# Products with V of a group's last 52 keys: two stationary tiles in place of three, and new orders of work in blocks 1 to 6

## The chip, the cores and the metric

The kernel runs on one core of a Trainium2 chip. Its time is the device time of one execution in microseconds (us). TensorE (PE in the profile) multiplies matrices. VectorE (DVE), ScalarE (ACT) and GpSimd (POOL) do elementwise work. SyncE (SP) issues most of the DMAs. Each engine runs its own instructions in the order in which they are written, and a wait on a semaphore holds everything queued behind it on that engine.

## What is computed

A block of Flamingo in float32: `x` is 2 batches of 2048 rows of 512, the context is 2 batches of 77 keys.

```python
x = x + tanh(g_xattn) * xattn(layernorm(x), ctx, ctx, Wq, Wk, Wv, Wo)   # 16 heads of 32, 77 keys
x = x + tanh(g_ffn)   * ffn(layernorm(x), w_gate, w_up, w_down)         # silu(gate) * up, hidden 1536
# in xattn: q @ k.T * 32**-0.5, key k masked for query rows below k, softmax, @ v, @ Wo.T
```

## The kernel before

The 4096 rows are worked on in 8 blocks of 512 rows (n = 0 to 7), each of four tiles of 128 rows (t = 0 to 3). After the blocks comes the feed-forward part in four pairs of steps, which the change does not touch. A float32 operand is split into a high part, which ScalarE copies out of PSUM as fp32r, and a low part, the difference, which VectorE forms. A product takes three TensorE products: high by high, low by high, high by low (`CROSS`).

One step n of the attention interleaves three things on TensorE, in this order: scores of tile 0; `values` for four groups m of four heads (the product of V with the probabilities of block n-1); scores of tile 1; then for each tile the transposes of its probabilities in three pieces `p(n, t, r)`, r = 0, 1, 2; `o(t)`, the projection of `values` by Wo; and at the end `q(m)`, the queries of block n+1. Scores are computed in two units of eight heads; unit 0 is softmaxed by VectorE (`shift0`: largest, then the difference) and ScalarE (`exp0`), unit 1 by ScalarE straight out of PSUM with a bias (`largest1`, `offset1` on VectorE, then eight instructions `exp1`). VectorE then forms sums and reciprocals (`denominator0`, `denominator1`), and GpSimd multiplies by them (`weigh`). Only then can TensorE transpose.

The eight heads of a unit have 616 keys in a row. They are transposed in five chunks, the third of which holds the last 52 keys of the even group and the first 52 of the odd group. A group's product with V therefore has three chunks, each with three TensorE products: nine per group, 36 per block. The pieces r of a transposed tile are chunks 0 to 3, 4 to 7 and 8 to 9 of the ten of both units. Piece r = 2 is 128 x 256 and is copied by one ScalarE instruction (`p_high`, L780) and subtracted by one VectorE instruction (`p_low`, L1070), which then frees the bank (`t_free`). `values` (L1646) waits for `t_free` before it reads the pieces: group 0 for all but the last two pieces of block n-1, group 1 for all but the last, groups 2 and 3 for all.

Two PSUM banks alternate for `values`, `o` and `q` (`m_wait`, semaphore `m_free`), two for the transposes (`t_wait`, `t_free`). `values` of group m + 2 waits until `weighted(m)` on ScalarE and `v_low(m)` on VectorE have emptied its bank, and `o(3)` waits for `residual(1)` on VectorE.

The orders of ScalarE, VectorE and GpSimd in a step are written out by hand (`step` at L882 and L1296, `block` at L630). Steps 1 to 6 share them, steps 0 and 7 have their own (`first_block`, `last_step`). Layer-norm statistics of later blocks (`stats`, `stats2`) are placed among VectorE's work by `st(i)`: in step 1 eight of them for blocks 2 and 3, in steps 2 to 5 four, in step 6 eight for the feed-forward part.

V is built in block 0. SyncE issues small DMAs, one for each entry of `V_PLACES` and batch, that put 25 to 77 rows of V where their chunk has them (L424). `v_high(b)` on ScalarE (L764) waits for all DMAs of its batch. In `first_block` of ScalarE `v_high(1)` stands between `p(2, 2)` and `q(2)`, and `p(3, 0)` comes behind `q(2)`.

At the end of step 7 ScalarE does `p(3, 0)`, `xv_copy`, `p(3, 1)`, `b12_copy`, `p(3, 2)`, and TensorE goes on with `values` for block 7.

## Time and profile before

| | |
|---|---|
| median of 3 runs | 872.54 us (872.40 to 872.73) |
| the profiled execution | 872.86 us, of which the span of the profile is 871.0 us |
| PE busy | 855.0 us, 98% |
| DVE, ACT, POOL busy | 653.3 us (75%), 461.1 us (53%), 403.1 us (46%) |

The page gives the busy time of each engine, the span in 40 slices, and the chain of work that ended last, followed back from the last instruction. The trace gives each instruction with its start and length, and behind it in brackets how long its engine stood idle before it and what ended that. A line of the timeline can merge instructions that follow each other on the engine (x2, x12); its length is then that of the whole.

### The profile page before, as it was taken

The page shows a single profiled execution, that of the slowest core. Times are in us where ns is not written, and L with a number is a line of the kernel's source. Part 1 is how long each engine was busy: PE and PEld are TensorE (multiplying, and loading weights), DVE is VectorE, ACT ScalarE, POOL GpSimd, SP SyncE. Part 2 cuts the span into 40 slices and gives each one's busy share as a digit, 9 for nine tenths or more (in the row PEclk, how much of TensorE's full clock was granted, in tenths as well). Part 3 has the DMA queues.
Part 4 walks back from the last instruction along what each step waited for, and adds up shares of the span by engine and source line. Part 5 has one row for each costly group of instructions (what it writes and reads, how often), then busy time and mean ns, then how long its engine had stood idle before and what let it go on. Part 6 is the DMA issues. An engine that isn't in the chain of part 4 may idle for free.

```text
span 871.0 us, 12870 instructions
## 1 busy us (share of the span) xinstructions
PE 855.0 (98%) x4087; PEld 706.8 (81%) x4087; DVE 653.3 (75%) x1081; ACT 461.1 (53%) x1130; POOL 403.1 (46%) x344
## 2 busy tenths in 40 slices
PE   8999999999999999999999999999999999999997
PEld 6678888888888887888888888888888888888876
DVE  5988877777786878679688478788487887587882
ACT  5787575756666757546056265165363364461550
POOL 4664555555565665437144444155253256151250
PEclk9999999999999999999999999999999999999999
DMA  9233847272728131567333256043275143243202
GB/s 329 78 107 121 270 153 253 84 241 85 242 97 277 48 133 38 212 234 266 116 120 135 97 187 248 14 165 122 74 247 187 48 164 107 96 171 117 90 38 98
DMA packets 60406, 128.73 MB, mean 148 GB/s; under 512 B 7616, under 2 KB 20416, under 8 KB 60352
## 3 DMA queue, kind: packets, MB, share of 16 engines
q1 hardware_dynamic: 58960, 125.95, 41.9%
q10 hardware_dynamic: 1392, 2.10, 0.7%
q8 instruction: 29, 0.48, 0.2%
q14 instruction: 25, 0.20, 0.1%
HBM read 99.93 MB, written 27.79 MB: 147 GB/s over the span
## 4 chain that ended last, share of the span: by engine, by line
PE 86%; DVE 6%; ACT 3%; issue 1%; DMA 1%; POOL 1%; ACTq 0%; DVEq 0%
PE psum L1880 34%; PE psum L1591 20%; PE psum L1930 18%; PE psum L1660 9%; PE psum L1616 4%; DMA xs<-x_t 1%; PE psum L1704 1%; ACT e L800 1%; POOL hT L705 1%; DVE bn L1055 1%; DVE K L1149 1%; DVE mx L1105 1%; DVE e L1097 0%; DVE qT L1079 0%; DVE mx L1094 0%
## 5 line engine op out<-in xcount | busy, mean ns | idle before, releaser
L1880 PE MATMUL psum<-xv,ring 128*128 128x512 f32 x1344 | 308.0, 390 | 1.0 <-ACT a L985 0.7
L1880 PEld LDWEIGHTS psum<-xv,ring 128*128 128x128 f32 x1344 | 251.3, 188 | 55.1 <-ACT a L985 1.1
L705 POOL TENSOR_TENSOR hT<-th,hT 128x512 fp32r<-128x512 f32 x48 | 86.7, 1806 | 200.7 <-ACT hT L1005 200.7
L1930 PE MATMUL psum<-w_d,hT 128*128 128x512 f32 x768 | 177.7, 390 | 1.3 <-POOL hT L705 0.8
L1930 PEld LDWEIGHTS psum<-w_d,hT 128*128 128x128 f32 x768 | 143.6, 188 | 32.7 <-POOL hT L705 2.0
L554 POOL TENSOR_TENSOR e<-e,rden 128x616 f32<-128x616 f32 x64 | 78.0, 1219 | 110.4 <-DVE rden L1131 75.2
L800 ACT ACTIVATE e<-psum,nmx,q_scale 128x77 f32<-128x77 f32 x256 | 102.9, 428 | 3.1 <-DVE nmx L1111 3.1
L973 ACT ACTIVATE a<-psum 128x512 f32<-128x512 f32 x48 | 28.7, 599 | 131.6 <-PE psum L1880 131.4
L1471 DVE SCALAR_TENSOR_TENSOR acc<-psum,gate_ffn,acc 128x512 f32<-128x512 f32 x64 | 47.6, 749 | 65.1 <-PE psum L1930 65.1
L1660 PE MATMUL psum<-wo,aT 128*128 128x512 f32 x384 | 95.5, 398 | 0.5 <-DVE aT L1079 0.5
L1591 PE MATMUL psum<-xT,wq 128*128 128x512 f32 x360 | 89.1, 398 | 0.4 <-DVE qT L1079 0.4
L1660 PEld LDWEIGHTS psum<-wo,aT 128*128 128x128 f32 x384 | 69.8, 188 | 14.3 <-DVE aT L1079 0.8
L1591 PEld LDWEIGHTS psum<-xT,wq 128*128 128x128 f32 x360 | 65.5, 188 | 14.7 <-DVE qT L1079 1.9
L705 POOL TENSOR_TENSOR hT<-c,hT 128x512 fp32r<-128x512 f32 x48 | 62.3, 1297 | 22.2 <-ACT hT L1005 22.2
L1591 PE MATMUL psum<-pT,V 128*128 128x512 f32 x288 | 68.0, 392 | 0.6 <-DVE aT L1079 0.6
L773 ACT ACTIVATE pT<-psum 128x512 fp32r<-128x512 f32 (+1 forms) x96 | 49.7, 534 | 33.9 <-PE psum L1616 33.9
L1591 PE MATMUL psum<-K,qT 128*128 128x308 f32 x384 | 63.9, 310 | 0.9 <-ACT e L800 0.9
L1591 PEld LDWEIGHTS psum<-pT,V 128*128 128x128 f32 x288 | 53.3, 188 | 12.5 <-DVE aT L1079 1.1
L1435 DVE SCALAR_TENSOR_TENSOR th<-th,c 128x512 f32<-128x512 f32 x48 | 56.1, 1168 | 7.1 <-ACT th L998 4.3
L1591 PEld LDWEIGHTS psum<-K,qT 128*128 128x128 f32 x384 | 56.9, 188 | 5.4 <-ACT e L800 1.8
L1005 ACT ACTIVATE hT<-th 128x512 fp32r<-128x512 f32 x48 | 30.4, 633 | 54.2 <-DVE th L1448 54.2
L1068 DVE TENSOR_TENSOR pT<-psum,pT 128x512 fp32r<-128x512 f32 (+1 forms) x96 | 55.7, 588 | 2.6 <-ACT pT L773 0.9
(110 smaller groups left out, 1204.7 us busy)
## 6 DMA issues: line engine op xcount, KB each, us to landing
ring<-w_var SPq DMA_DIRECT2D x48, 896.0 KB, 4.6
w_var<-stage SPq DMA_DIRECT2D x12, 896.0 KB, 4.6
x_ln<-x SPq DMA_DIRECT2D x32, 256.0 KB, 4.7
x_res<-x SPq DMA_DIRECT2D x32, 256.0 KB, 5.2
x_mid<-x_res SPq DMA_DIRECT2D x32, 256.0 KB, 2.0
x<-x_mid SPq DMA_DIRECT2D x16, 512.0 KB, 5.6
acc<-x_mid SPq DMA_DIRECT2D x16, 512.0 KB, 6.2
out<-acc SPq DMA_DIRECT2D x32, 256.0 KB, 2.0
```

What stands on the lines that cost most here:

```text
L554: nc.gpsimd.tensor_tensor(e[:, t % 2, hs], e[:, t % 2, hs], rden[:, t % 2, hs].unsqueeze(2).to_broadcast([P, UH, SK]), ALU.mult).then_inc( ...
L705: nc.gpsimd.tensor_tensor(hT[:, 1, i % HH, j, :], h[:, :], hT[:, 0, i % HH, j, :].bitcast(f32), ALU.subtract).then_inc(h_lo, 1)
L773: nc.scalar.activation(dst, src, ACT.Copy).then_inc(t_hi, 1)
L800: last = nc.scalar.activation(e[:, t % 2, UH + h, :], s_bank[1][:, h // HG, (h % HG) * SK:(h % HG + 1) * SK], ACT.Exp, bias=nmx[:, t % 2, ...
L1068: nc.vector.tensor_tensor(dst, src, hi.bitcast(f32), ALU.subtract).then_inc(t_free, 1)
L1435: nc.vector.scalar_tensor_tensor(th2[:, :], th2[:, :], 1.0, c22[:, :], ALU.add, ALU.mult)\
L1471: nc.vector.scalar_tensor_tensor(acc[:, t, :], m_bank[t % 2][:, :], gate_ffn[:, 0:1], acc[:, t, :], ALU.mult, ALU.add).then_inc(m_free, 1)
L1591: last = nc.tensor.matmul(dst, stat, mov, start=(j == 0), stop=(j == len(terms) - 1))
L1616: last = nc.tensor.transpose(t_bank[at % 2][:, j * P:(j + 1) * P], rows[:, start:start + P], ident[:, :])
L1660: last = nc.tensor.matmul(m_bank[t % 2][:, :], aT[:, a, m, t * P:(t + 1) * P], wo[:, c, m, :], start=m == 0 and a + c == 0, stop=m == G - ...
L1880: last = nc.tensor.matmul(psum[:, bank, :], stat, mov, start=start and j == 0, stop=j == len(terms) - 1, skip_group_check=not start)
L1930: last = nc.tensor.matmul(m_bank[t % 2][:, :], hT[:, a, m, t // TT, (t % TT) * P:(t % TT + 1) * P], w_d[:, HH * h + m, :], start=m == 0 an ...
```

## The change

Chunk 2 of a unit is moved so that its 128 keys straddle the border of the two groups at row 64: it starts at key 244 in place of 256. Rows 0 to 63 then belong to the even group (52 keys of it count) and rows 64 to 127 to the odd one. A new tile `pR` holds for each group both parts of its half in one operand of 128 rows: the high part in the rows of the half itself, the low part in the other 64 rows. The rows of V for the 52 keys are written twice, 64 rows apart. One product of V's high part and one of V's low part with `pR` then stand in place of three (the term low by low is added by it). A group takes eight products in place of nine.

`p_high` and `p_low` of piece 2 become two instructions each, of 64 rows by 256. The pieces r = 0 and 1 now hold the four full chunks of unit 0 and of unit 1, and r = 2 the two shared ones. Each group of `values` first waits for the piece of its own unit, does six products, then waits for the last piece of the block, and does two. `V_PLACES` has 14 entries in place of 12, as the program computes them. The orders of ScalarE, VectorE and GpSimd in steps 1 to 6 are others; the order of TensorE and the orders of steps 0 and 7 stay.

```diff
-    SH = 2 * (GK - 2 * P)
-    CS = [0, P, 2 * P, 2 * P + SH, 3 * P + SH]
+    HP = P // 2
+    CS = [0, P, GK - HP, HK - 2 * P, HK - P]
...
+            pR = sb("pR", [P, 2, 2, TB], f32r, c1)
...
+                            if at == CU // 2:
+                                row, key, rows = places[-1][3:]
+                                places.append((odd, c, j, (row + HP) % P, key, rows))
...
             def block(n, ahead, first=False):
-                probabilities(n, 0)
-                x_low_t(n + 1, (0, 1))
+                weigh(n, 0, 0)
+                x_low_t(n + 1, (0,))
+                weigh(n, 0, 1)
                 probabilities(n, 1)
-                x_low_t(n + 1, (2, 3))
-                probabilities(n, 2)
+                x_low_t(n + 1, (1, 2))
+                weigh(n, 2, 0)
+                x_low_t(n + 1, (3,))
+                weigh(n, 2, 1)
...
             def p_high(n, t, r, at):
+                for odd in range(2):
+                    rows = slice(odd * HP, odd * HP + HP)
+                    last = nc.scalar.activation(pR[rows, :, odd, c], src[rows], ACT.Copy)
+                last.then_inc(t_hi, 1)
...
             def step(n):                                   (ScalarE)
+                x_high_t(n + 1, 0)
+                weighted(n, 0)
                 exp0(n, 0)
-                weighted(n, 0)
-                exp1(n, 0, lambda: weighted(n, 1))
+                weighted(n, 1)
+                exp1(n, 0)
                 weighted(n, 2)
                 weighted(n, 3)
-                for k in range(KD):
+                for k in range(1, KD):
                     x_high_t(n + 1, k)
+                p(n, 0, 0)
+                p(n, 0, 1)
+                exp1(n, 1, lambda: exp0(n, 1))
+                p(n, 0, 2)
...
             def p_low(n, t, r, at):
+                for odd in range(2):
+                    rows = slice(odd * HP, odd * HP + HP)
+                    other = slice((1 - odd) * HP, (1 - odd) * HP + HP)
+                    last = nc.vector.tensor_tensor(pR[other, :, odd, c], src[rows], pR[rows, :, odd, c].bitcast(f32),
+                                                   ALU.subtract)
+                last.then_inc(t_free, 1)
...
             def step(n, ahead):                            (VectorE)
+                def st(place):
+                    if ahead and not (isinstance(n, int) and n == 1):
+                        if place in (0, 3, 4, 6):
+                            stats(n + 2, (0, 3, 4, 6).index(place))
+                    elif ahead:
+                        stats(2 + place // TT, place % TT)
+                    else:
+                        stats2(place // TT, place % TT)
+                largest0(n, 0)
+                largest1(n, 0)
                 slot_free(n, 0)
-                shift(n, 0)
+                below0(n, 0)
+                offset1(n, 0)
+                v_low(n, 0)
+                sum0(n, 0)
+                v_low(n, 1)
+                inverse0(n, 0)
+                st(0)
+                denominator1(n, 0)
+                v_low(n, 2)
+                v_low(n, 3)
+                st(1)
+                largest1(n, 1)
                 slot_free(n, 1)
+                offset1(n, 1)
+                largest0(n, 1)
                 p(n, 0, 0)
+                below0(n, 1)
+                p(n, 0, 1)
                 denominator0(n, 1)
+                denominator1(n, 1)
                 residual(n, 0)
                 p(n, 0, 2)
+                st(2)
                 slot_free(n, 2)
                 shift(n, 2)
                 p(n, 1, 0)
+                residual(n, 1)
...
             def values(i, m, b, split):
+                u, odd = divmod(m, 2)
+                pe.wait_ge(t_free, split - 2 + u)
+                m_wait(i)
+                for c in range(2):
+                    for a, d in CROSS:
+                        nc.tensor.matmul(m_bank[m % 2][:, :], V[:, B - 1 - b, a, 3 * m + odd + c, :],
+                                         pT[:, d, 2 * m + c, :], start=c == 0 and a + d == 0, stop=False)
                 pe.wait_ge(t_free, split)
+                for a in range(2):
+                    last = nc.tensor.matmul(m_bank[m % 2][:, :], V[:, B - 1 - b, a, 3 * m + 2 - 2 * odd, :],
+                                            pR[:, u, odd, :], start=False, stop=a == 1)
...
-                values(M_LAST + m, m, B - 1, T_P2 - 2 + min(m, 2))
+                values(M_LAST + m, m, B - 1, T_P2)
```

## Rows read from the trace of the kernel before

**Rows 1.** The page: busy time of the engines, share of the span, instructions.
```profile
PE 855.0 (98%) x4087; PEld 706.8 (81%) x4087; DVE 653.3 (75%) x1081; ACT 461.1 (53%) x1130; POOL 403.1 (46%) x344
```

**Rows 2.** Timeline of PE, start and length: first scores of blocks 1, 2, 3, 6, 7.
```profile
61.20 1.97 PE L1591 MATMUL psum<-K,qT 128*128 128x308 f32 x12
...
103.42 2.12 PE L1591 MATMUL psum<-K,qT 128*128 128x308 f32 x12
...
146.16 2.12 PE L1591 MATMUL psum<-K,qT 128*128 128x308 f32 x12
...
272.13 2.11 PE L1591 MATMUL psum<-K,qT 128*128 128x308 f32 x12
...
313.65 2.11 PE L1591 MATMUL psum<-K,qT 128*128 128x308 f32 x12
```

**Rows 3.** Timeline of block 3: the products with V, and DVE's first steps beside them.
```profile
147.95 0.79 DVE L1094 TENSOR_REDUCE mx<-psum 128x8 f32<-128x616 f32 x1
...
148.12 8.35 PE L1591 MATMUL psum<-pT,V 128*128 128x512 f32 x36
...
148.78 0.86 DVE L1097 TENSOR_TENSOR e<-psum,mx 128x308 f32<-128x308 f32 x2
...
150.46 0.23 DVE L1111 SCALAR_TENSOR_TENSOR nmx<-mx,q_scale,minus 128x8 f32<-128x8 f32 x1
```

**Rows 4.** Timeline of SP (DMA issues) in block 0; median us to landing of two kinds.
```profile
33.46 10.65 SPq L424 DMA_DIRECT2D v_first<-v_keys  x12
44.16 10.43 SPq L424 DMA_DIRECT2D v_late<-v_keys  x12
...
x_mid<-x_res SPq DMA_DIRECT2D x32, 256.0 KB, 2.0
```

**Rows 5.** Stretches of block 0: engines' busy time, PE clock, DMA share, GB/s.
```profile
54.40:54.80 0.40, 0.40 (x4) 0.31 (x3) 0.40 (x2) 0.40 (x5) 0.40 (x1) 1.00 0.19 27
54.80:55.20 0.40, 0.40 (x4) 0.31 (x3) 0.40 (x2) 0.40 (x5) 0.05 (x1) 1.00 0.02 1
```

**Rows 6.** Timeline of ACT, DVE and PE at the end of block 0.
```profile
56.99 1.55 ACT L764 ACTIVATE V<-v_late 128x1536 fp32r<-128x1536 f32 x1
...
59.52 0.60 ACT L773 ACTIVATE pT<-psum 128x512 fp32r<-128x512 f32 x1 [0.49 <-PE psum L1616]
...
60.89 0.44 PE L1616 MATMUL psum<-ident,e 128*128 128x128 f32 x2 [0.85 <-DVE pT L1068]
```

**Rows 7.** Timeline, 32-row instructions in a row, and 128-row ones behind them.
```profile
18.18 2.62 DVE L1149 TENSOR_TENSOR K<-psum,K 32x154 fp32r<-32x154 f32 x8
20.84 1.29 DVE L1079 TENSOR_TENSOR qT<-psum,qT 128x512 fp32r<-128x512 f32 x2
...
17.57 2.43 ACT L757 ACTIVATE K<-psum 32x154 fp32r<-32x154 f32 x8
```

**Rows 8.** Groups by line and form: busy us, mean ns of one.
```profile
L1068 DVE TENSOR_TENSOR pT<-psum,pT 128x256 fp32r<-128x256 f32 x32 | 13.5, 421 | 1.7 <-ACT pT L773 0.2
L1055 DVE BATCH_NORM_STATS2 bn<-x_ln 128x6 f32<-128x512 f32 x32 | 21.7, 679 | 0.0
```

**Rows 9.** Timeline of PE in block 2: products with V of groups 2 and 3.
```profile
109.91 4.68 PE L1591 MATMUL psum<-pT,V 128*128 128x512 f32 x18 [0.27 <-DVE aT L1079]
```

**Rows 10.** Timeline of block 7, where exp1 of tile 1 ends.
```profile
332.38 0.90 ACT L773 ACTIVATE pT<-psum 128x256 fp32r<-128x256 f32 x2
...
332.81 1.18 DVE L1068 TENSOR_TENSOR pT<-psum,pT 128x256 fp32r<-128x256 f32 x2
...
333.91 0.74 DVE L1141 SCALAR_TENSOR_TENSOR x_res<-psum,gate_t,x_res 128x512 f32<-128x512 f32 x1
```

**Rows 11.** Timeline at the end of step 7: last pieces, last products with V.
```profile
350.05 4.34 PE L1591 MATMUL psum<-pT,V 128*128 128x512 f32 x18
...
351.51 0.39 ACT L773 ACTIVATE pT<-psum 128x256 fp32r<-128x256 f32 x1
...
351.94 0.42 DVE L1068 TENSOR_TENSOR pT<-psum,pT 128x256 fp32r<-128x256 f32 x1 [0.19 <-ACT pT L773]
```

More of the change, by code:

```diff
@@ L300, in v_places @@
                 for c in range(3):
-                    start = CS[2 * odd + c]
+                    at = 2 * odd + c
                     for j in range(HG):
                         first = (odd * HG + j) * SK
-                        lo = max(first, start)
-                        hi = min(first + SK, start + (SH if 2 * odd + c == 2 else P))
+                        lo = max(first, CB[at])
+                        hi = min(first + SK, CE[at])
                         if lo < hi:
-                            places.append((odd, c, j, lo - start, lo - first, hi - lo))
+                            places.append((odd, c, j, lo - CS[at], lo - first, hi - lo))
+                            if at == CU // 2:
+                                row, key, rows = places[-1][3:]
+                                places.append((odd, c, j, (row + HP) % P, key, rows))
             return places
         V_PLACES = v_places()
-        P_PARTS = ((0, 4), (4, 4), (8, 2))
         def too_wide(eng):
@@ L893, in q, with rest @@
                     m_high(q_at + m, m, qT[:, 0, m, :])
-                for t in (1, 2):
-                    p(n, t - 1, 0)
-                    exp0(n, t)
-                    p(n, t - 1, 1)
-                    exp1(n, t)
-                    p(n, t - 1, 2)
+                x_high_t(n + 1, 0)
+                weighted(n, 0)
+                exp0(n, 0)
+                weighted(n, 1)
+                exp1(n, 0)
+                weighted(n, 2)
+                weighted(n, 3)
+                for k in range(1, KD):
+                    x_high_t(n + 1, k)
+                p(n, 0, 0)
+                p(n, 0, 1)
+                exp1(n, 1, lambda: exp0(n, 1))
+                p(n, 0, 2)
+                p(n, 1, 0)
+                p(n, 1, 1)
+                exp0(n, 2)
+                exp1(n, 2)
+                p(n, 1, 2)
                 p(n, 2, 0)
+                p(n, 2, 1)
+                q(0)
                 exp0(n, 3)
-                p(n, 2, 1)
-                exp1(n, 3, lambda: q(0))
-                p(n, 2, 2)
-                q(1)
+                def rest():
+                    p(n, 2, 2)
+                    q(1)
+                exp1(n, 3, rest)
                 q(2)
@@ L1100, in shift0 @@
                 last.then_inc(s0_shifted, 1)
+            def shift0(n, t):
+                largest0(n, t)
+                below0(n, t)
             def largest1(n, t):
@@ L1611, in transpose_p @@
                 rows = e[:, t % 2].rearrange("p h k -> p (h k)")
-                first, parts = P_PARTS[r]
-                for j in range(parts):
-                    u, c = divmod(first + j, CU)
-                    start = u * HK + CS[c]
+                starts = [r * HK + CS[c] for c in FULL] if r < 2 else [u * HK + CS[CU // 2] for u in range(2)]
+                for j, start in enumerate(starts):
                     last = nc.tensor.transpose(t_bank[at % 2][:, j * P:(j + 1) * P], rows[:, start:start + P],
@@ L1790, in weigh_values @@
                 for m in range(G):
-                    values(m_base(n) + m, m, b_before, t_base(n) - 2 + min(m, 2))
+                    values(m_base(n) + m, m, b_before, t_base(n))
             def step(n, b, b_before, masked):
```

91 lines of the change are left out of this document (38 added, 53 removed).

## The prediction
> **What bounds the kernel now.** I read the page first: PE is busy 98% of the span, the next engine, DVE, 75% [rows 1]. So a product taken away is worth its own length wherever nothing else is late. Then the timeline of PE, for where each block starts [rows 2]: block 1 takes 42.22 us, block 2 42.74, block 3 41.85, block 6 41.52; blocks 4 and 5 lie between. The waits inside a block are a few tenths. Last I followed the timelines of DVE and ACT at four places where PE does wait or could: the end of block 0, the start of block 2, block 7, and the last products with V.
>
> **What is removed.** Each group has one product less. 36 take 8.35 us, 0.232 each [rows 3]; less the tail of the last one it is 0.231. Four per block are 0.93 us, 32 in all 7.4 us. That is the most the change can give. It is a gain only where PE is the last to be ready.
>
> **The halves of piece 2.** A half has 64 rows but the same 256 elements in a row. On DVE 128 rows of 256 elements take 0.42 us [rows 8] and of 512 take 0.69, two of these back to back 1.29, so that they overlap by 0.09 [rows 7]. By that line 154 elements take 0.31. Eight DVE instructions of 154 elements and only 32 rows, which change their start row each time, take 2.62, 0.33 each, and ACT's eight 2.43, 0.30 each [rows 7]. So the number of rows doesn't count, the row's length does, and a change of start row takes the overlap away. Each half costs what the whole did, 0.42 on DVE and 0.39 on ACT [rows 8, 11]. The halves change their start row from 0 to 64 and back. So DVE gets 0.33 net of an overlap and loses three overlaps of 0.09, 0.6 us per tile, and ACT about 0.5. The lower bound is the overlapped length, 0.33 us on either; below nothing it can't be, since instructions are added. I take the upper end, as the 32-row rows are the nearest. The Trainium skill ("VectorE: DVE Perf Modes", section "Two Vector instructions with no wait between them") says that a Vector instruction whose start quadrant differs from the last one read or written starts only when all earlier ones have finished. This speaks against the change; by it DVE pays the 0.6, without it 0.33, and the trace's eight instructions agree with it for DVE.
>
> **Block 0: V's DMAs.** V's places go from 12 to 14 per batch. Twelve issues took 10.65 and 10.43 us [rows 4], 0.87 each, so the last issue of `v_late` starts four issues, 3.5 us, later: it began at 44.16 + 10.43 − 0.87 = 53.7 and now does at 57.2. The last traffic ended by about 54.8 [rows 5], 1.1 after that issue began, so it now ends by 58.3; a DMA to memory takes 2.0 from issue [rows 4], which gives 59.2, and with the issue itself 60. `v_high(1)` ran at 56.99 without a wait [rows 6]; it now waits until 58.3 to 60, I take 58.9. Behind it on ACT stand `q(2)` and `p(3, 0)`. The latter began 2.53 after `v_high(1)`, of which 0.49 was a wait for PE that now goes; PE began `p(3, 2)` 1.37 after it. So PE goes on 2.53 − 0.49 + 1.37 = 3.4 after `v_high(1)`, at 62.3 in place of 60.89: +1.4 us. Landing at 58.3 gives 0.8, at 60 2.5, and 0.4 is the added halves alone, which hold ACT until 57.9 if V is there earlier. ACT's added halves lie under that wait otherwise. The Trainium skill ("DMA: Bandwidth & Descriptors", section "Anatomy of one DMA — SWDGE (gpsimd) path") has a fixed cost of about 2.0 us per DMA; by it alone, with landing at 59.2, the term would be +1.7.
>
> **Blocks 3 to 5.** I walked the new orders with the lengths of the trace, from the first scores on. `values` starts at 2.0, its last group ends at 9.4 and `o(0)` starts at 12.0. On DVE the last halves end at 2.4 (1.8 before, and 0.6), in time for the two held-back products of group 0 at 2.0 + 6 × 0.231 = 3.4. Two reductions of 0.79, the differences 0.86, the offset 0.23 [rows 3] and `v_low(0)` 0.69, less overlaps, then end at 5.6; group 2 wants that bank at 2.0 + 16 × 0.231 = 5.7 with 0.15 for the semaphore. That is the tightest place: 0.1 us of stall. `residual(1)` ends at 23.0, wanted by `o(3)` at 23.3. `weigh(0, 1)` on POOL ends at 11.2, wanted at 11.5. In the second half the slack is over 1 us. Two small waits of before, for `p(2, 2)` and `q(2)`, go (0.1 to 0.2). POOL's weight build now waits for the last statistics, but ends 3.5 us ahead of its next `weigh`. So a block takes 41.0 for 41.85: −0.85 each, −2.5 for three (−3.2 with no stall, −1.5 with 0.45 in each).
>
> **Blocks 1 and 6** have eight statistics, one at each `st`, two of them, `st(1)` and `st(2)`, between `v_low(3)` and `p(1, 0)`. One is 0.68 [rows 8] and its aggregate, 0.8 to 1.0 together. In blocks 3 to 5 that stretch has 0.3 us to spare ahead of `o(3)`. The first one delays `exp0(1)`, which the new order puts amid `exp1(1)`, the second comes on top: `residual(1)` ends 1.4 (block 6) or 1.7 us later, and PE stalls ahead of `p(1, 2)` and `o(3)` for 1.2 and 1.5. Block 6: 42.2 for 41.52, +0.6 (−0.9 if hidden, +1.0). Block 1: 42.65 for 42.22, +0.4 (−0.6 to +1.0).
>
> **Block 2** starts behind block 1's statistics. Before, PE waited for `v_low(0)` ahead of group 2, which began at 109.91, and again ahead of group 3: 18 products took 4.68 for the 4.2 of their lengths [rows 9]. Now the chain to `v_low(0)` is 0.6 longer by the halves, and PE's two groups ahead of it are 0.46 shorter: group 2 waits 1.15 us, and group 3 no more, since `v_low(1)` no longer stands amid `exp1`. 42.2 for 42.74: −0.5 (−1.0 to 0).
>
> **Block 7** keeps its order, and PE isn't its bound. From the end of `exp1(1)` the chain goes through ACT's `p(0, 2)` and `p(1, 0)`, 0.90 for both, DVE's low parts, 1.18, then `residual(0)` at 333.91, and the largest and the offset that release `exp1(2)` [rows 10]. The added half on ACT (0.4) and on DVE (0.4) both stand on it: +0.8, and the same behind `exp1(2)`: +1.6 for both (0.7 if overlapped). At the block's start the halves delay `v_low(0)` by 0.6, against 0.46 saved in groups 2 and 3: +0.1. Together +1.7 (0.4 to 2.2).
>
> **The last products with V.** Before, groups 0 and 1 ran from 350.05 without a wait, while `p(3, 2)` was copied at 351.51 and subtracted at 351.94 [rows 11]. Now group 0's last two products need it: PE, which has its pace from 350.3 on, is there after six products, 1.39 us, at 351.7. The two halves on ACT end at 352.45, on DVE at 353.35, and PE goes on at 353.5: a stall of 1.8. Two groups then save 0.46 of it, the other two 0.46 more, and VectorE's `form` standing ahead of the last `v_low` gives back some 0.3: +1.2 (0.5 to 1.6).
>
> **The sum.** +1.4 +0.4 −0.5 −2.5 +0.6 +1.7 +1.2 = +2.3 us; the feed-forward part, 0. The profiled execution would be 872.86 + 2.3 = 875.2, of it 1.86 outside the span. The median of the runs lies 0.3 lower, so 874.8.
>
> **The rivals.**
> - *The halves overlap.* Speaks for it: two waits stand between most DVE instructions anyhow and they overlap there; against it, rows 7. Then block 0 is +1.0, block 1 +0.2, block 7 +0.85, the end +0.95: and with block 2 at −0.5, 3 to 5 at −2.5 and 6 at +0.5 the sum is +0.5. Time 873.0, no change. Chance 0.28.
> - *The new orders have more cover than my walk gives them.* If also blocks 1 and 6 don't stall (the walk adds some forty lengths, and 0.3 us per link decides): block 0 +0.7, block 1 −0.6, block 2 −0.8, blocks 3 to 5 −3.0, block 6 −0.9, block 7 +0.6, the end +0.9 = −3.1. Time 869.4, faster. This decides if `residual(1)` keeps 1.2 us of slack. PE bound throughout, −7.4, 865.1, is part of it, at 0.03. Chance together 0.22.
> - *Every block stalls at group 2.* `v_low(0)` has 0.1 us; if each length in that chain is 0.1 longer, the four blocks 2 to 5 lose 0.5 each: 876.7. Inside the forecast's side. Chance 0.12.
> That four products fewer per block are executed is fixed by the code, and is no rival.
>
> **How the numbers follow.** Forecast 874.8, chance 0.38. All low ends together give −4.4, all high ends +6.8; the range leaves the two corners out: 869.4, the fast rival, to 877.6. A measurement of this kernel tells 0.2%, 1.7 us, from no change: 874.3 and 870.8 are the bounds. Slower: 0.38 and 0.12, 0.50; same 0.28; faster 0.22. The forecast case's own range is 873.5 to 877.
>
> **What would show it.** In the profile after: 28 issues of V, and an idle time of ACT ahead of `v_high(1)`; 256 products with V; the halves at 0.4 each on both engines and without overlap; blocks 3 to 5 at 41.0 us; PE waiting for `x_res` ahead of `o(3)` in blocks 1 and 6; a wait of 1.8 us within the first group of the last products. It would be wrong if V lands by 58, if the halves overlap, or if no wait for `x_res` shows.

## The result: 875.65 us for 872.42

| | before | after |
|---|---|---|
| median | 872.42 us (872.39 to 872.73, 7 runs) | 875.65 us (874.07 to 876.08, 7 runs) |
| ratio of the runs | | 1.0031, 95% interval 1.002 to 1.0043 |
| the profiled execution | 872.86 us, span 871.0 | 876.08 us, span 874.3 |
| PE busy, products | 855.0 us, 4087 | 850.2 us, 4055 |
| DVE, ACT busy | 653.3, 461.1 us | 668.0, 475.3 us |

The changed kernel is slower by 0.3%. PE has 32 products less, as the change says, and 4.8 us less of busy time; DVE and ACT have 14.7 and 14.2 us more. The page of the kernel after, where [rows 1] stood:

```profile
PE 850.2 (97%) x4055; PEld 702.1 (80%) x4055; DVE 668.0 (76%) x1113; ACT 475.3 (54%) x1162; POOL 401.7 (46%) x344
```

The halves and the products, from the groups by line and form (busy us, mean ns of one, idle time before them):

```profile
L1107 DVE TENSOR_TENSOR pR<-psum,pR 64x256 fp32r<-64x256 f32 x64 | 27.0, 422 | 3.3 <-ACT pR L798 1.9
L798 ACT ACTIVATE pR<-psum 64x256 fp32r<-64x256 f32 x64 | 24.3, 380 | 1.3 <-PE psum L1670 1.0
L1707 PE MATMUL psum<-pT,V 128*128 128x512 f32 x192 | 50.8, 400 | 2.1 <-DVE aT L1114 2.1
L1711 PE MATMUL psum<-pR,V 128*128 128x512 f32 x64 | 20.1, 395 | 1.5 <-DVE pR L1107 1.5
```

A half costs 422 ns on DVE, as much as the whole piece did (421 [rows 8]).

Where each block starts, timeline of PE of the kernel after (blocks 1, 2, 3, 7 and the feed-forward part; what [rows 2] showed of before):

```profile
62.66 2.68 PE L1647 MATMUL psum<-K,qT 128*128 128x308 f32 x12
...
107.09 1.10 PE L1647 MATMUL psum<-K,qT 128*128 128x308 f32 x6 [0.17 <-issue]
...
148.74 2.12 PE L1647 MATMUL psum<-K,qT 128*128 128x308 f32 x12
...
313.83 1.46 PE L1647 MATMUL psum<-K,qT 128*128 128x308 f32 x7
...
375.20 1.07 PE L1940 MATMUL psum<-xv,ring 128*128 128x512 f32 x4
```

From such lines I made a table for every kernel that ran: the time from a block's first scores to the next block's, block 7 with the last products up to the first product of the feed-forward part ("FF"). All are of the profiled executions.

| kernel | block 1 starts | 1 | 2 | 3 | 4 | 5 | 6 | 7 and last | FF starts |
|---|---|---|---|---|---|---|---|---|---|
| before | 61.20 | 42.22 | 42.74 | 41.85 | 42.24 | 41.88 | 41.52 | 58.19 | 371.84 |
| after | 62.66 | 44.43 | 41.65 | 40.86 | 41.04 | 40.84 | 42.35 | 61.37 | 375.20 |
| e1, V's copy late | 61.30 | 43.56 | 41.65 | 40.86 | 41.11 | 40.84 | 42.45 | 61.33 | 373.10 |
| e2, bridge | 62.78 | 42.80 | 41.71 | 40.86 | 41.08 | 40.83 | 42.32 | 61.32 | 373.70 |
| e3, old orders | 62.73 | 44.81 | 45.90 | 44.51 | 44.55 | 44.49 | 44.09 | 61.27 | 392.35 |
| e4, halves alone | 61.29 | 45.13 | 45.91 | 44.74 | 44.84 | 44.73 | 44.25 | 60.62 | 391.51 |
| e5, orders alone | 60.88 | 41.99 | 41.59 | 41.59 | 41.93 | 41.52 | 41.88 | 58.16 | 369.54 |
| e6, orders and halves | 61.30 | 43.01 | 42.08 | 41.60 | 41.92 | 41.52 | 42.56 | 60.56 | 374.55 |
| e7, halves, statistics moved | 61.17 | 43.25 | 43.99 | 43.06 | 43.14 | 43.08 | 42.65 | 60.54 | 380.88 |
| e8, e1 and GpSimd waits | 61.62 | 42.81 | 41.65 | 40.87 | 41.09 | 40.86 | 42.34 | 61.27 | 372.51 |
| e9, column halves | 61.38 | 42.45 | 43.46 | 42.65 | 43.02 | 42.64 | 41.52 | 58.44 | 375.56 |
| e10, e5 and edits | 61.08 | 41.84 | 41.59 | 41.59 | 41.93 | 41.55 | 41.86 | 56.64 | 368.08 |
| e11, e8 and edits | 62.06 | 41.48 | 41.77 | 40.87 | 41.09 | 40.82 | 41.12 | 58.60 | 367.81 |
| e12, e11 and last products | 61.38 | 41.43 | 41.78 | 40.86 | 41.08 | 40.82 | 41.14 | 58.08 | 366.57 |

Before and after: +1.46 in block 0, +2.21, −1.09, −0.99, −1.20, −1.04, +0.83, +3.18. The sum is +3.36, and the feed-forward part takes as long as before. Of the last +3.18, 2.22 lie in block 7 (first scores to the first of the last products: 36.40 us before, from 313.65 to 350.05, and 38.62 after, from 313.83 to 352.45) and 0.96 in the last products.

The lines behind the losses. At the end of block 0 the DMAs of V land late: the chain that ended last (start, us, what), then ACT's and PE's timeline.

```profile
55.90 0.76 SPq L430
56.66 0.04 issue
56.71 2.08 DMA v_late<-v_keys
```

```profile
58.81 1.49 ACT L773 ACTIVATE V<-v_late 128x1536 fp32r<-128x1536 f32 x1 [1.57 <-DMA v_late<-v_keys]
...
62.30 0.44 PE L1670 MATMUL psum<-ident,e 128*128 128x128 f32 x2 [2.02 <-DVE pT L1094]
```

The fourteenth DMA lands at 58.79, 2.08 us after its issue began at 56.71; ACT waits 1.57 for it, and PE 2.02 ahead of `p(3, 2)`, where it had waited 0.85 [rows 6]. Then, in stretches of 1 us (busy time of PE, PEld, DVE, ACT, POOL, then PE's granted clock, DMA share, GB/s):

```profile
62.00:63.00 1.00, 0.70 (x4) 0.55 (x5) 1.00 (x3) 0.61 (x2) 1.00 (x1) 1.00 1.02 256
63.00:64.00 1.00, 1.00 (x8) 1.00 (x7) 0.85 (x2) 0.96 (x3) 0.83 (x1) 0.80 0.96 318
64.00:65.00 1.00, 1.00 (x6) 1.00 (x5) 0.93 (x3) 0.20 (x1) 0.00 (x0) 0.50 1.04 398
65.00:66.00 1.00, 1.00 (x5) 0.81 (x4) 1.00 (x2) 0.00 (x0) 0.00 (x0) 0.50 0.88 300
66.00:67.00 1.00, 1.00 (x4) 0.81 (x3) 1.00 (x4) 0.00 (x0) 0.00 (x0) 0.50 1.10 329
67.00:68.00 1.00, 1.00 (x6) 0.82 (x5) 0.08 (x1) 0.00 (x0) 0.00 (x0) 1.00 0.89 247
```

A granted clock of 0.50 is the level of 1.2 GHz. Before, it was 1.00 in each of these stretches. The first scores of block 1 take 2.68 us here for 1.97 [rows 2]. In the seven executions of the kernel after, the mean granted clock was 0.996 or 0.997 in four, which took 875.65 to 876.08 us, and 0.999 in the three that took 874.07 to 874.48. Only the first of them has a trace, and it is one of the four.

The waits of PE in block 1, at the head of block 7, in its tiles and in the last products (start, length, group, and in brackets the idle time and what ended it):

```profile
88.27 0.44 PE L1670 MATMUL psum<-ident,e 128*128 128x128 f32 x2 [0.76 <-DVE pT L1094]
88.93 3.02 PE L1720 MATMUL psum<-wo,aT 128*128 128x512 f32 x12 [0.22 <-DVE x_res L1191]
```

```profile
321.23 1.62 PE L1707 MATMUL psum<-pT,V 128*128 128x512 f32 x6 [1.51 <-DVE aT L1114]
...
346.85 0.66 PE L1670 MATMUL psum<-ident,e 128*128 128x128 f32 x4 [1.42 <-POOL e L560]
...
352.45 1.62 PE L1707 MATMUL psum<-pT,V 128*128 128x512 f32 x6
355.62 0.73 PE L1711 MATMUL psum<-pR,V 128*128 128x512 f32 x2 [1.55 <-DVE pR L1107]
```

Block 6 has the pair ahead of `p(1, 2)` and `o(3)` too (0.61 and 0.22); group 2 waits 0.57 in block 2 and 1.51 in block 7.

The idle time in brackets is less than what a stall costs, because TensorE products that follow each other without a wait overlap in the timeline, and a stall takes that overlap away too. From the scores of tile 2 to those of tile 3 it is 9.91 us in block 1 (81.87 to 91.78) and 9.71 in block 6 (289.22 to 298.93), where block 5, without these stalls, has 8.32 (248.38 to 256.70). So the pair costs 1.6 us in block 1 and 1.4 in block 6.

### The profile page after: what moved, and what is told of

Read it like the earlier page. It is cut to its first block, busy times and chain, and to the rows that moved or that the text cites. A ratio compares the mean times of both kernels' runs of the same rounds, so it can differ in the third digit from the quotient of the medians.

```text
span 874.3 us, 12880 instructions
## 1 busy us (share of the span) xinstructions
PE 850.2 (97%) x4055; PEld 702.1 (80%) x4055; DVE 668.0 (76%) x1113; ACT 475.3 (54%) x1162; POOL 401.7 (46%) x344
## 4 chain that ended last, share of the span: by engine, by line
PE 80%; DVE 8%; ACT 4%; SPq 3%; issue 2%; DMA 1%; POOL 1%; ACTq 0%; DVEq 0%
PE psum L1940 34%; PE psum L1990 19%; PE psum L1647 10%; PE psum L1720 8%; PE psum L1707 4%; SPq L430 3%; PE psum L1670 2%; ACT e L817 2%; PE psum L1711 1%; DMA xs<-x_t 1%; PE psum L1764 1%; DVE pR L1107 1%; DVE bn L1081 1%; DVE pT L1094 1%; DVE qT L1114 1%
## 5 line engine op out<-in xcount | busy, mean ns | idle before, releaser
L1670 PE MATMUL psum<-ident,e 128*128 128x128 f32 x320 | 47.3, 275 | 8.1 <-DVE pT L1094 3.8
L817 ACT ACTIVATION_READ_ACCUMULATOR e<-psum,nmx,q_scale 128x1 f32 x256 | 55.0, 215 | 0.0
L782 ACT ACTIVATE pT<-psum 128x512 fp32r<-128x512 f32 x64 | 36.6, 610 | 29.9 <-PE psum L1670 29.8
L1707 PE MATMUL psum<-pT,V 128*128 128x512 f32 x192 | 50.8, 400 | 2.1 <-DVE aT L1114 2.1
```

What stands on the lines that cost most here:

```text
L782: nc.scalar.activation(dst, src, ACT.Copy).then_inc(t_hi, 1)
L817: last = nc.scalar.activation(e[:, t % 2, UH + h, :], s_bank[1][:, h // HG, (h % HG) * SK:(h % HG + 1) * SK], ACT.Exp, bias=nmx[:, t % 2, ...
L1670: last = nc.tensor.transpose(t_bank[at % 2][:, j * P:(j + 1) * P], rows[:, start:start + P], ident[:, :])
L1707: nc.tensor.matmul(m_bank[m % 2][:, :], V[:, B - 1 - b, a, 3 * m + odd + c, :], pT[:, d, 2 * m + c, :], start=c == 0 and a + d == 0, stop= ...
```

## The experiments

All medians have their runs of the kernel before beside them (872.35 to 872.68).

### What of the change costs, and what brings

Four kernels, together with before and after, take the change apart: the old orders put back (e3), the halves alone (e4), the new orders alone (e5), orders and halves (e6).

e3 puts the `step` of ScalarE and VectorE and the `block` of GpSimd of the kernel before into the kernel after. e4 edits the kernel before, `p_low` as shown and `p_high` likewise:

```diff
 def p_low(n, t, r, at):
...
+                for odd in range(2):
+                    rows = slice(odd * 64, odd * 64 + 64)
+                    last = nc.vector.tensor_tensor(pT[rows, 1, 8:10, c], src[rows],
+                                                   pT[rows, 0, 8:10, c].bitcast(f32), ALU.subtract)
```

> The products, the halves and V's places of the change, but ScalarE, VectorE and GpSimd take the orders of the kernel before in blocks 1 to 6. My theory: the old orders leave v_low(0) 0.6 us later in blocks 2 to 6 while PE comes 0.46 earlier to group 2, so that blocks 3 to 5 take 41.4 each in place of 40.9 and block 2 about 42.2, while blocks 1 and 6 lose the stalls at x_res (-1.0 each): in sum 0 to +1.5 us against the changed kernel, 875.7 to 877. The rival, that the orders bring nothing and the products alone the gain: blocks 3 to 5 at 40.9, blocks 1 and 6 shorter by 1.0, 873.7.

> The kernel before, all its products and orders kept, but piece 2 of p_high and p_low is done as two instructions of 64 rows in place of one of 128 rows: the price of the halves alone. Theory: a half costs as much as the whole, 0.38 on ScalarE and 0.42 on VectorE, and the two don't overlap. So block 7 gets 0.77 per tile twice, 1.6, plus 0.6 at group 2; blocks 2 to 6 get 0 to 0.6 each at group 2; the last products nothing, since PE gets there after 18 products; block 0 +0.3. In sum +3 to +4: 875.5 to 876.5. The rival, that they overlap: +0.7 in block 7 and nothing elsewhere, 873.2.

Measured: e3 894.73 us (ratio 1.0251, 1.0237 to 1.0265), e4 892.42 us (1.0225, 1.0211 to 1.0239). Both expectations were far off: the halves alone cost 20 us, 17 of them in blocks 1 to 6 (2.6 to 3.2 in each, where I had allowed 0 to 0.6) and 2.4 in block 7. The place is in VectorE's timeline of block 3. The offset `nmx` of the four tiles, in the kernel before:

```profile
150.46 0.23 DVE L1111 SCALAR_TENSOR_TENSOR nmx<-mx,q_scale,minus 128x8 f32<-128x8 f32 x1
160.24 0.23 DVE L1111 SCALAR_TENSOR_TENSOR nmx<-mx,q_scale,minus 128x8 f32<-128x8 f32 x1
168.87 0.23 DVE L1111 SCALAR_TENSOR_TENSOR nmx<-mx,q_scale,minus 128x8 f32<-128x8 f32 x1
177.41 0.23 DVE L1111 SCALAR_TENSOR_TENSOR nmx<-mx,q_scale,minus 128x8 f32<-128x8 f32 x1
```

and in e4, with two of the steps between:

```profile
157.18 0.23 DVE L1129 SCALAR_TENSOR_TENSOR nmx<-mx,q_scale,minus 128x8 f32<-128x8 f32 x1
166.84 0.23 DVE L1129 SCALAR_TENSOR_TENSOR nmx<-mx,q_scale,minus 128x8 f32<-128x8 f32 x1
...
171.32 0.86 DVE L1090 TENSOR_TENSOR pT<-psum,pT 64x256 fp32r<-64x256 f32 x2 [0.43 <-ACT pT L790]
172.21 0.69 DVE L1064 BATCH_NORM_STATS2 bn<-x_ln 128x6 f32<-128x512 f32 x1
...
176.44 0.23 DVE L1129 SCALAR_TENSOR_TENSOR nmx<-mx,q_scale,minus 128x8 f32<-128x8 f32 x1
185.96 0.23 DVE L1129 SCALAR_TENSOR_TENSOR nmx<-mx,q_scale,minus 128x8 f32<-128x8 f32 x1
```

From the second to the third and on to the fourth it was 8.63 and 8.54 us and is 9.60 and 9.52. The old order is a loop over the tiles: `nmx` lets ScalarE's `exp1` start (3.2 us); behind it, in ScalarE's order, comes piece 2 of the tile before; VectorE waits for it, and behind it, in its order, come a statistic, a residual, two reductions and the difference, and the next `nmx`. Each half that is added stands on that loop on both engines: the pair takes 0.86 on DVE for 0.42, and 0.79 on ACT for 0.43. That is 0.80 of the 0.97 and 0.98 us. The loop had no slack to cover it, since its 8.63 and 8.54 were already a little more than PE's time for a tile, 8.34 and 8.32 between the scores of tiles 1, 2 and 3 (156.30, 164.64 and 172.96).

e3 has the same halves and 32 products fewer, and its blocks 3 to 5 are only 0.23 to 0.29 us shorter than those of e4. Where the loop is the bound, less work for TensorE brings little. Four of e3's five executions took 894.21 to 894.89 us with a mean clock of 0.998 or 0.999, the traced one 893.21 with 1.000, so some 1 us of its median can be the clock; those four have no trace.

e5 and e6 have the new orders and all the old products; e6 has the halves as well.

> The kernel before with its own products, its whole piece 2 and its twelve places of V, and only the new orders of ScalarE, VectorE and GpSimd in blocks 1 to 6. Theory: PE has as much work as before and sets the pace in blocks 3 to 5 (41.8 each, against 41.85 to 42.24), block 2 gains 0.5 of its waits, blocks 1 and 6 pay 0.5 each for the statistics ahead of p(1, 0): 871.5 to 872.7. The orders bring nothing by themselves; they are the cover of the halves. Rival: the new orders are faster by themselves, and the products were worth less than 0.93 a block: under 871.

> The run before this one and the two instructions of 64 rows for piece 2, so all of the change except the products left out and V's added places. Theory: under the new orders the halves cost nothing in blocks 3 to 5 (41.9 each, where under the old orders they cost 3.2 a block), 0.5 in block 2 and 0.5 each in blocks 1 and 6, 0.4 at the end of block 0, 0.77 twice and some 0.6 at group 2 in block 7, nothing in the last products: 874.5 to 875.5. Then the products left out are worth about 0.93 in each of blocks 1 to 6, less than 7.4 in all, and what the changed kernel loses again lies in block 0 and the last products. Rival: the halves cost in blocks 3 to 5 too, and the products' gain hid it: over 877.

Measured: e5 870.53 us (0.998, 0.9971 to 0.9989), e6 875.62 us (1.0036, 1.0023 to 1.005). The orders bring 1.9 us by themselves, 1.15 of it in block 2: that is the rival, in its time (under 871) and, as e6 shows, in what it says of the products (0.68 to 0.88 in blocks 3 to 5, less than 0.93). With them the halves cost nothing in blocks 3 to 5 (41.60, 41.92, 41.52 for 41.59, 41.93, 41.52); they cost 0.4 in block 0, 1.0 in block 1, 0.5 in block 2, 0.7 in block 6 and 2.4 in block 7: 5.0, where my terms add up to 4.0. So in terms of where the feed-forward part starts: orders −2.3 (371.84 to 369.54; 0.3 of it in block 0, where the trace of before happened to start later), halves +5.0 (to 374.55), fewer products and V's added places +0.65 (to 375.20). The last of these is −2.9 in blocks 2 to 6 (0.43, 0.74, 0.88, 0.68, 0.21) against +1.4 in block 0, +1.4 in block 1, and +0.8 in block 7 and the last products. The +1.4 in block 1 is the clock, as e2 shows below (+1.6); without it the products left out bring 0.2 there.

e7 is a test of the loop; `st(1)` is moved behind `shift(n, 3)` in the same way:

```diff
                 p(n, 0, 2)
-                st(0)
                 residual(n, 1)
                 slot_free(n, 2)
                 shift(n, 2)
+                st(0)
                 p(n, 1, 0)
```

> The kernel before with the halves alone (892.42 us), and one thing more: VectorE's statistics st(0) and st(1), 0.68 with 0.18 for the aggregate each, stand behind shift(n, 2) and shift(n, 3) and not ahead of them. Theory: the old order is a loop, from the offset nmx of a tile through exp1 on ScalarE, piece 2 of the tile before on ScalarE and VectorE, the statistics, the residual and the largest to the next offset; it took 8.54 us a tile before (168.87 to 177.41), just as long as PE's work, and 9.52 with the halves. With 0.86 of statistics out of it, it takes 8.7, and the blocks 2 to 6 go from 45 back to about 42.5 us: 877 to 879. Rival: it is VectorE's total work or group 2's wait that costs, and the place of the statistics is without effect: 890 to 892.

Measured: 882.01 us (1.0112, 1.0096 to 1.0127). VectorE keeps all its work, and 10.4 of the 20 us are gone, so it isn't the engine's load. The two links take 8.51 and 8.47 (`nmx` at 162.89, 171.40, 179.87), a little less than the 8.7 expected:

```profile
162.89 0.23 DVE L1129 SCALAR_TENSOR_TENSOR nmx<-mx,q_scale,minus 128x8 f32<-128x8 f32 x1
171.40 0.23 DVE L1129 SCALAR_TENSOR_TENSOR nmx<-mx,q_scale,minus 128x8 f32<-128x8 f32 x1
179.87 0.29 DVE L1129 SCALAR_TENSOR_TENSOR nmx<-mx,q_scale,minus 128x8 f32<-128x8 f32 x1
```

But block 3 takes 43.06 and not 42.5: from the last `nmx` to the next block it is now 11.60 for 10.60 before and 11.11 in e4, and 0.56 are lost ahead of the first `nmx`, as in e4. So of the 2.89 us that the halves alone cost in block 3, the two links have 1.95, and moving the statistics takes 2.14 out of them. What stands ahead of the first `nmx` and behind the last has the rest. The loop is shown by this run; that the moved statistic is what adds 0.49 behind the last `nmx` follows from its place in the order and was not tested.

e9 asks what makes a pair of halves expensive. In it piece 2 is split by columns, not by rows: two instructions of 128 x 128.

> The kernel before, old orders and all its products, with piece 2 of p_high and p_low again as two instructions, but of 128 rows and 128 elements each, so that the start row stays. Beside the run with 64-row halves (892.42 us) it tells whether the number of instructions or the change of the start row costs. Theory: with the start row unchanged the two overlap. On VectorE 512 elements take 0.69 and 256 take 0.42, so 128 take some 0.28, two of them less 0.09 are 0.47 in place of 0.42; ScalarE likewise 0.4 to 0.5. The loop of a tile gets 0.1 and not 0.86: 872.5 to 874.5. Rival: two instructions don't overlap whatever their rows, 0.56 to 0.6 for two on each engine: 876 to 880.

Measured: 875.75 us (1.0037, 1.0024 to 1.0051), between the two expectations. The pairs, timeline of DVE and ACT:

```profile
165.53 0.49 DVE L1086 TENSOR_TENSOR pT<-psum,pT 128x128 fp32r<-128x128 f32 x2
```

```profile
165.01 0.49 ACT L788 ACTIVATE pT<-psum 128x128 fp32r<-128x128 f32 x2
```

One takes 284 ns on DVE and 308 on ACT, so two overlap by 0.08 and 0.13. Two of 64 rows take 0.86 on DVE for 2 × 0.422, and 0.76 to 0.79 on ACT for 2 × 0.380: no overlap. So two instructions as such aren't what costs. The pairs differ in their rows (64 and 128) as well as in the start row, and no run has two halves of 64 rows with one start row; that the start row is the reason rests on this pair and on the 32-row rows of before [rows 7], where eight instructions don't overlap either. The Trainium skill ("VectorE: DVE Perf Modes", section "Two Vector instructions with no wait between them") has such a rule for VectorE; both pairs agree with it.

The total was 1.3 us above my range, for two reasons. The two links of block 3 take 8.75 and 8.67 for 8.63 and 8.54 before, 0.12 and 0.13 more, which is just what the pairs add on the two engines (0.49 for 0.42, and 0.49 for 0.43). This much I had expected. The larger part, 0.55 of the 0.80 us in block 3, lies behind the last `nmx`, which took 0.75 us and ended with an instruction of GpSimd (timelines of DVE and POOL):

```profile
178.79 0.75 DVE L1125 SCALAR_TENSOR_TENSOR nmx<-mx,q_scale,minus 128x8 f32<-128x8 f32 x1
```

```profile
178.78 0.74 POOL L627 TENSOR_TENSOR stage<-stage 128x256 fp32r<-128x256 f32 x1
```

The same `nmx` takes 0.75 or 0.76 in blocks 2, 4 and 5, and 0.23 in the kernel before. Without these four times 0.52 us the run would be at about 873.7 (an estimate from these rows), inside the range. The shift of a few tenths brought VectorE's instruction onto one of GpSimd's; e1 and e8 below show the same with a longer one.

### The end of block 0 and the clock

```diff
                 p(2, 2)
-                v_high(1)
                 q(2)
                 p(3, 0)
                 q(3)
                 p(3, 1)
                 p(3, 2)
+                v_high(1)
```

> The changed kernel, but in block 0 ScalarE copies the second batch of V behind p(3, 2), not ahead of q(2). My theory is that two costs hang on that copy: PE's idle 2.02 us ahead of p(3, 2), which the late landing of V makes, and the stretch after it in which the granted clock stood at 0.50 (63.5 to 67 us), worth 1.6 us of block 1. Then block 1's first scores start at 60.7 in place of 62.66, block 1 takes 42.8 in place of 44.43, no stretch of block 1 has a granted clock under 0.95, and the time is 3.3 us below the changed kernel's 875.65: 872.3. If the clock falls for another reason than the idle time, only the wait goes: 873.9, with the 0.50 stretch still there. If the wait was covered by something else that is as late, it stays near 875.6.

e2 leaves that copy where it is and gives PE something to do while it waits:

```diff
                 p(3, 1)
+                pe.wait_ge(s0_shifted, 4)
+                for _ in range(8):
+                    nc.tensor.matmul(s_bank[0][:, 0, 0:P], ident[:, :], ident[:, :], start=True, stop=True)
                 p(3, 2)
```

> The changed kernel, with eight more products of 128 x 128 on TensorE ahead of p(3, 2) in block 0, into a bank whose contents nobody reads any more; they fill some 1.7 of the 2.02 us in which PE stood idle there and do nothing else. The wait for V stays: first scores of block 1 at 62.7. If the idle time is what made the clock fall, the stretch from 63 to 67 us has 1.00, block 1 takes 42.8 in place of 44.43, and the time is 874.05 in every run, the lower of the changed kernel's two levels. If the clock falls whatever PE does there, the time stays at 875.65 and block 1 at 44.4.

Measured: e1 874.27 us (1.0017, 1.0008 to 1.0026), e2 874.73 us (1.0023, 1.0014 to 1.0032). In e2 the granted clock is 1.00 in every stretch from 60 to 70 us, block 1 starts at 62.78 and takes 42.80 for 44.43, and the eleven runs lie between 874.36 and 874.86, near the lower level of the kernel after and without its upper one. The eight products in the gap (timeline of PE; each is two records), and a stretch of 1 us in which the kernel after had 0.50:

```profile
60.26 1.95 PE L1845 MATMUL psum<-ident 128*128 128x128 f32 x16
62.48 0.44 PE L1670 MATMUL psum<-ident,e 128*128 128x128 f32 x2 [0.27 <-DVE pT L1094]
```

```profile
64.00:65.00 1.00, 1.00 (x8) 0.96 (x7) 0.93 (x4) 0.38 (x1) 0.04 (x1) 1.00 1.02 393
```

So with the gap filled this fall did not come in eleven executions, where it came in some four of seven without, and it is worth 1.6 us. The gap makes the fall possible but doesn't bring it each time: in the profiled execution of e3 PE stood idle just as long and the clock stayed.

```profile
62.42 0.44 PE L1652 MATMUL psum<-ident,e 128*128 128x128 f32 x2 [2.03 <-DVE pT L1082]
62.73 1.97 PE L1629 MATMUL psum<-K,qT 128*128 128x308 f32 x12
```

This gap seems not to be the only place where the clock can fall. e11 and e12 below have V's copy late and wait only 0.8 us there, and one execution of each stands out all the same, 869.61 us at a mean clock of 0.997 and 869.38 at 0.996, 1.3 and 1.7 us above the medians. They have no trace, so where the clock fell, if it did, is open.

e1 has the long wait and the fall gone (0.75 for 2.02), and gained only half of what I expected. Two new things took the rest: the wait there doesn't go to zero, it goes back to what it was before the change; and group 2 of block 1 now waits 1.09 us. Timeline of DVE and POOL of e1:

```profile
65.50 1.83 DVE L1153 SCALAR_TENSOR_TENSOR nmx<-mx,q_scale,minus 128x8 f32<-128x8 f32 x1
67.25 0.68 DVE L1114 TENSOR_TENSOR aT<-psum,aT 128x512 fp32r<-128x512 f32 x1
```

```profile
63.80 3.50 POOL L579 TENSOR_TENSOR V<-v_late,V 128x1536 fp32r<-128x1536 f32 x1 [3.67 <-ACT V L773]
```

`nmx`, 0.22 us elsewhere, took 1.83 and ended at 67.33, with GpSimd's pass over V (67.30). e8 tests that: GpSimd's pass waits for `nmx_ready` of that tile.

> The changed kernel with V's second copy at the end of ScalarE's block 0 (874.27 us), and GpSimd's low part of it waits until the offset of block 1's first tile is formed. In the run with the copy alone that offset took 1.83 us in place of 0.22 and ended with GpSimd's pass over V (67.33 and 67.30), and PE waited 1.09 at group 2. Theory: VectorE's small instruction from SBUF to SBUF waits for a GpSimd instruction under way, so with the pass behind it the 1.09 goes: block 1 takes 42.5 in place of 43.56, 873.2. Rival: the offset waited for its inputs, or the later pass delays weigh(1, 0, 0) and so p(0, 0) as much: 874.3.

Measured: 873.52 us (1.0013, 1.0004 to 1.0022). `nmx` takes 0.22 again (at 65.86), GpSimd's pass starts behind it (66.16), the wait at group 2 is gone, and block 1 takes 42.81. A new wait of 0.34 for GpSimd ahead of tile 0's transposes is as long as what is missing from the expected 873.2. The Trainium skill ("SBUF — State Buffer", section "Who interferes with whom") says that a DVE instruction with two inputs in SBUF and a GpSimd instruction that reads SBUF exclude each other; `nmx` has two such inputs, `mx` and `minus`, and the trace agrees with its 1.83 against 0.22.

### A better version

e10 is e5, e11 is e8, both with these edits, and in both block 7 begins in the order of the other blocks; e12 is e11 with one more, shown further down. Of the statistics the diff has the new places only.

```diff
 # VectorE, blocks 1 and 6: statistics where it stood idle
                 st(0)
+                st(1)
...
                 residual(n, 1)
+                st(2)
...
                 st(4)
+                st(5)
                 q(1)
+                st(6)
 # VectorE, block 7: the next tile's offset here, the residual later, behind the next p(n, t - 1, 1)
                     p(n, t - 1, 2)
                     p(n, t, 0)
                     if t + 1 < TT:
-                        residual(n, t - 1)
+                        largest1(n, t + 1)
+                        offset1(n, t + 1)
 # ScalarE, end of block 7
                 p(n, 3, 1)
-                b12_copy(0)
                 p(n, 3, 2)
+                b12_copy(0)
```

> The kernel before with the new orders alone (870.53 us) and these edits of order, no other products and no halves: in blocks 1 and 6 the statistics stand where VectorE was idle (st(1) behind st(0), st(2) behind residual(n, 1), st(5) behind st(4), st(6) behind q(1)); block 7 begins as the other blocks do; in its tiles the largest and the offset of the next tile come ahead of the residual; ScalarE's p(3, 2) stands ahead of b12_copy. Theory: 0.2 at x_res, 0.7 at the head of block 7 (waits of 0.34 and 0.34), and 0.65 in each of two tiles of block 7, the residual's length in the loop: 868.3. Rival: PE is the bound of block 7's tiles too, and only 0.9 of it comes: 869.6.

> The changed kernel with V's second copy late on ScalarE and GpSimd (873.52 us) and the same edits of order as the run before this. Theory: 0.8 in block 1 (waits of 0.58 and 0.22 ahead of p(1, 2) and o(3)), 0.6 at group 2 of block 2, 0.9 in block 6, 1.0 at group 2 of block 7, 0.65 in each of two tiles of block 7, and 0.9 in the last products, where p(3, 2) no longer waits for b12_copy: 5.5 in all, 868.0, about level with the run before, since the halves still cost in block 7 what the fewer products bring. Rival: with PE 0.93 shorter in every block, VectorE becomes the bound of blocks 1 to 6, and less than 3 of it comes: over 870.5.

Measured: e10 869.25 us (0.9964, 0.9951 to 0.9978), e11 868.27 us (0.9956, 0.9943 to 0.997). In e11 the tiles of block 7 take 6.63 us (327.88 to 334.51) for 7.28, 0.65 less as expected; in e10 6.13 (329.88 to 336.01) for 6.51. So e10, expected at 868.3, came nearer to its rival's 869.6. e11 gained 5.25 us of the 5.5 expected: block 1 gives 1.3, block 6 1.2, block 7 and the last products 2.7; block 2 gives nothing, group 2 waits 0.61 there as before.

e12 changes the last products, and on VectorE puts `xv_low(0, B11)` behind `p(3, 2)`:

```diff
+            values_whole(M_LAST, 0, B - 1, T_P2)        # six products of group 0
+            values_whole(M_LAST + 1, 1, B - 1, T_P2)    # six of group 1
+            values_rest(0, B - 1, T_P2)
+            values_rest(1, B - 1, T_P2)
```

> The changed kernel with the edits of order (868.27 us), and in the last products with V TensorE runs the six products of groups 0 and 1 that need no halves first, then the two and two that need them; on VectorE xv_low(0, B11) stands behind p(3, 2). There TensorE waited 1.02 us behind group 0's first six products, for the halves of p(3, 2). Theory: this wait is all that the held-back products cost there, and group 1's six products, 1.4 us, cover it: first of the last products to the feed-forward's first product goes from 22.2 (345.60 to 367.81) to 21.2, 867.2. Rival: the next in line, v_low of group 0 ahead of group 2, comes as late as before, and the wait turns up there: 868.2.

Measured: 867.64 us (0.9949, 0.9935 to 0.9963). The wait of 1.02 is gone and one of 0.63 stands at group 2 for `v_low(0)` (350.23), which is the rival in part: the time lies midway between the 867.2 and the 868.2, and from the first of the last products to the feed-forward part it is 21.74 for 22.21. This is the fastest kernel of the study, 4.9 us below its runs of before. Of these, e10 has 3.1 without the halves and without the fewer products.

## Why the prediction was right, point by point

874.8 was predicted, 875.65 measured, within the range of 869.4 to 877.6 and on the side of "slower", by 0.31%. The sum was +2.3 and is +3.36. The path was right in most terms; one cost, the clock, was not in the sum at all. Its terms:

| term | predicted | measured |
|---|---|---|
| block 0 | +1.4 | +1.46 |
| block 1 | +0.4 | +2.21 |
| block 2 | −0.5 | −1.09 |
| blocks 3 to 5 | −2.5 | −3.23 |
| block 6 | +0.6 | +0.83 |
| block 7 | +1.7 | +2.22 |
| last products | +1.2 | +0.96 |
| sum | +2.3 | +3.36 |

- *Block 0.* The mechanism was as predicted: `v_high(1)` at 58.81 (58.9), PE's `p(3, 2)` at 62.30 (62.3). The profiled execution was 0.5 us ahead of the one before by then (TensorE's products with `wk` began at 10.70 for 11.18, as soon as it had landed), so the end of block 0 itself cost about 1.9. e1 shows 1.4 of it by the copy's place. The DMAs of V landed 2.08 us after the issue, near the 2.0 of [rows 4]; the section of the Trainium skill that the prediction names beside it ("DMA: Bandwidth & Descriptors", section "Anatomy of one DMA — SWDGE (gpsimd) path") is on DMAs that GpSimd issues, and these are issued by SyncE, so the trace's number is the one to go by.
- *Block 1* is the term that failed. The stalls at `p(1, 2)` and `o(3)` are there and cost 1.6 us for the 1.5 I gave. What I left out is that a longer wait of PE can cost more than its length: the granted clock. e2 sizes it, 1.6 us, which is nearly all of the miss (+0.58 without it, within my bounds of −0.6 to +1.0).
- *Block 2* waited 0.57 for group 2 and not 1.15, so it gained 0.6 more.
- *Blocks 3 to 5* took 40.86, 41.04 and 40.84 for 41.0. The mis-sized step is small: I took 0.85 off each block of about 41.9, and block 4 was longer than the others before (42.24). e5 and e6 divide it: 0.26 to 0.36 of each is the new orders' own, for the 0.1 to 0.2 that I gave to the waits at `p(2, 2)` and `q(2)`, and 0.68 to 0.88 of the 0.93 of the products arrives. The 0.93 itself is a little high: by their starts (148.12 to 156.30) the 36 products of block 3 take 0.227 each, and four of them 0.91. In block 5 some 0.2 more is lost around group 2, the place I had called the tightest: the groups start at 232.59, 234.42, 236.30 and 238.25 and end at 240.08, so that two of them take 1.88 and 1.95 for 1.83.
- *Block 6*, within its bounds, with the two stalls at the place predicted; they cost 1.4 for 1.2.
- *Block 7.* 7.28 us a tile for 6.51 is +0.77, twice, for the 0.8 and 0.8 of the prediction. e6 against e5 gives the halves 2.4 there, and in e11 the edits of order take 0.65 of the 0.77 out of a tile again. The size that was wrong is the head of the block: group 2 waits 1.51 us for 0.34 before, and up to the scores of tile 1 it takes 11.40 us for 10.77, +0.63 where I had +0.1.
- *The last products* waited 1.55 for the 1.8 predicted, at the place predicted, and cost 0.96 for 1.2.
- *The halves* cost 0.422 and 0.380 and don't overlap, as the 32-row rows [rows 7] had let expect. e9 agrees with the reason: with the start row kept, a pair overlaps.

Two misses of opposite sign, +1.8 in block 1 and −1.3 in blocks 2 to 5, leave a sum that is better than its terms. That is luck. So is the side: the executions in which the clock seems not to have fallen took 874.07 to 874.48 us, right at the 874.3 that the prediction set as the border between "slower" and "no change". And I had not seen at all what the new orders do in the change: I walked them as they are, which was enough for a forecast, but didn't walk the old ones with the halves. So the 20 us of e4 are nowhere in the prediction.

The rivals: that the halves overlap fell, since a pair takes 0.86 us on DVE for 2 × 0.422. That the new orders have more cover came true in blocks 2 to 5 and not in 1, 6 and 7. That every block stalls at group 2 came true of its four blocks in block 2 alone, and in block 7, which it had left out.

## What to carry to other kernels

Before an instruction is split or added on an engine that is idle a quarter of the time, follow one small step (here the offset) from tile to tile and compare the distance with the bound engine's time per tile: if they are equal there is no slack, whatever the busy shares say, and the order must change with the split. Fewer products on the bound engine are worth their length only as far as the others keep up: under the new orders they brought 2.9 us in blocks 2 to 6, of the 4.6 that they are long there, and with what they cost at both ends of the attention part 0.65 in all. A wait of the bound engine should be kept short or filled, since here 2.0 us idle could cost 1.6 us more. And a small VectorE instruction that many others wait for should not fall onto a long one of GpSimd: a shift of a few tenths of a us was enough to bring that about in e9.

## What the runs showed of the hardware that I had not expected

- After TensorE had stood idle for 2.02 us its granted clock was 0.50, the 1.2 GHz level, from 64 to 67 us, though the engine was busy again from 62.3 on. In the traced execution of e3, with a wait of 2.03, it stayed at 1.00, and so it did in the trace of e2 with eight products in the gap.
- A VectorE instruction of 8 elements a row, 0.22 us, took 1.83 us, and ended within 0.03 of the end of a GpSimd instruction that was under way. Moving the GpSimd instruction brought it back to 0.22. In e9 the same instruction took 0.75 us beside a GpSimd instruction of 0.74 that had begun 0.01 ahead of it.
- On ScalarE, too, two instructions in a row of 64 rows that start at rows 0 and 64 don't overlap (0.76 to 0.79 for 2 × 0.380), while two of 128 rows that start at the same row do (0.49 for 2 × 0.308).
